# First expert stage: down product two chunks behind, a third hidden tile, waits per PSUM bank, and PSUM copies on ScalarE

## The reference

```python
shared_out = _swiglu(x, ws_gate, ws_up, ws_down)      # width 128
scores = sigmoid(x @ gate_weight.T)                   # 8 scores a token
topk_w, topk_idx = top_k(scores, 2)
topk_w = topk_w / (topk_w.sum(-1) + 1e-20) * 2.5
combine = einsum('tk,tke->te', topk_w, one_hot(topk_idx))
hmid = silu(x @ w_gate) * (x @ w_up)                  # 8 experts, width 64 each
out = einsum('te,teh->th', combine, hmid @ w_down) + shared_out
```

## Time and profile before

| | |
|---|---|
| runs of the kernel | 1990.7 us median of three (1988.94 to 1991.46) |
| profiled execution | 1989.05 us, of which the span of instructions is 1987.2 us |
| TensorE busy over the span | 81% |
| VectorE, ScalarE busy over the span | 71%, 50% |
| first experts in this execution | from 761.7 us, when its first ScalarE work starts, to 926.1 us, when its last statistics are done |
| mean granted TensorE clock over the span | 0.92 of full |

### The profile page before, as it was taken

How to read it: one execution, slowest core, us unless ns; L and a number is a source line. 1 busy time by engine, 2 the same in 40 slices (tenths; PEclk the granted TensorE clock), 3 DMA queues, 4 the chain that set the end, 5 groups by cost and what they waited for, 6 DMA issues and landing times. The chain is left out here.

```text
span 1987.2 us, 37884 instructions
## 1 busy us (share of the span) xinstructions
PE 1602.9 (81%) x11056; PEld 1044.5 (53%) x11056; DVE 1403.6 (71%) x3795; ACT 989.3 (50%) x2687; POOL 484.3 (24%) x503
## 2 busy tenths in 40 slices
PE   6999999999998997888967845776776433698998
PEld 3666666666664554555645744565665433243443
DVE  5777777777775665666864447999999855576775
ACT  3666666666663332333322258999999410111110
POOL 1111111111111010000001107888888551000000
PEclk9999999999999998998988977889888766799999
DMA  4111011110109100001660000000000000000000
GB/s 128 33 32 30 23 32 32 32 32 21 32 12 292 47 0 1 1 0 54 195 202 0 0 0 0 1 0 1 1 0 0 11 0 21 28 6 11 6 6 16
DMA packets 69349, 66.54 MB, mean 33 GB/s; under 512 B 5695, under 2 KB 66834, under 8 KB 69266
## 3 DMA queue, kind: packets, MB, share of 16 engines
q1 hardware_dynamic: 66598, 64.00, 10.7%
q10 hardware_dynamic: 2668, 1.62, 0.3%
HBM read 61.41 MB, written 4.19 MB: 33 GB/s over the span
## 5 line engine op out<-in xcount | busy, mean ns | idle before, releaser
L1962 PE MATMUL ss_y_ps<-ss_h,ss_diag 128*128 128x256 f32 x1024 | 266.1, 424 | 132.1 <-ACT sc_dt L1880 92.0
L1962 PEld LDWEIGHTS ss_y_ps<-ss_h,ss_diag 128*128 128x128 f32 x1024 | 217.2, 215 | 180.7 <-issue 93.9
L595 ACT ACTIVATE x_probs<-x_probs,x_neg_max 128x257 f32<-128x257 f32 x512 | 253.6, 498 | 63.2 <-DVE x_neg_max L696 63.2
L696 DVE CUSTOM_DVE_ANT_0 x_probs<-x_s_ps,x_mask_b 128x257 f32<-128x257 f32 x512 | 187.2, 422 | 132.6 <-PE x_s_ps L403 132.6
L1864 ACT ACTIVATE ss_decay<-sc_dt,sc_a 128x256 f32 (+1 forms) x496 | 207.1, 473 | 1.8 <-DVE ss_h L1927 1.8
L1918 DVE SCALAR_TENSOR_TENSOR ss_decay<-ss_decay,ss_h 128x1024 f32<-128x1024 f32 x124 | 152.3, 1228 | 29.3 <-ACT ss_decay L1864 29.1
L1874 ACT ACTIVATE ss_come<-ss_dtu,sc_xd 128x256 f32<-128x256 f32 x384 | 163.1, 507 | 6.6 <-POOL ss_dtu L1820 6.6
L1834 POOL TENSOR_TENSOR ss_diag<-all_ident,sc_xd 128x512 f32<-128x512 f32 x128 | 160.7, 1256 | 11.4 <-PE ss_y_ps L1962 1.4
L413 PE MATMUL x_pT_ps<-all_ident,x_probs 128*128 128x128 f32 x1024 | 162.0, 281 | 0.6 <-DVE x_pT L703 0.6
L703 DVE COPY x_pT<-x_pT_ps 128x512 f32<-128x512 f32 x256 | 161.2, 668 | 0.0
L1927 DVE CUSTOM_DVE_ANT_0 ss_h<-ss_come,ss_decay 128x1024 f32<-128x1024 f32 x124 | 149.9, 1209 | 0.0
(11 more groups left out here) (363 smaller groups left out, 3110.2 us busy)
## 6 DMA issues: line engine op xcount, KB each, us to landing
x_ctx_t<-ctxT SPq DMA_DIRECT2D x48, 514.0 KB, 3.8
kept_ctx_t<-ctxT SPq DMA_DIRECT2D x16, 514.0 KB, 7.9
kept_ctx_n<-ctx SPq DMA_DIRECT2D x16, 512.0 KB, 8.4
x_ctx_n<-ctx SPq DMA_DIRECT2D x16, 512.0 KB, 4.0
all_x<-x SPq DMA_DIRECT2D x4, 512.0 KB, 7.3
x_mid<-all_x SPq DMA_DIRECT2D x32, 64.0 KB, 3.8
all_x<-x_mid SPq DMA_DIRECT2D x4, 512.0 KB, 7.5
out<-all_x SPq DMA_DIRECT2D x8, 256.0 KB, 2.0
```

Source lines behind the costliest of these rows:

```text
L595: ins = nc.scalar.activation(probs[p][:, n, :], probs[p][:, n, :], ACT.Exp, scale=-1.0, bias=neg_max[p][:, n:n + 1], accum_out=sums[p][:, ...
L696: vec.tensor_tensor_reduce(probs[p][:, n, :], s_ps[:, c, 0:S2], mask_b[:, :], -1.0, -MASKED, ALU.add, ALU.min, neg_max[p][:, n:n + 1]).the ...
L1962: ins = nc.tensor.matmul(y_ps[p][:, 0:DI], diag[q][:, m, :], h[q][:, m, :], start=(q == 0 and m == 0), stop=(q == NQ - 1 and m == NH - 1))
```

## The change

- `project` stands two chunks behind (`LAG0 = 2`), and `hid` has three tiles.
- `up` is split into `gate_up` (G and U) and `weigh` (W). G raises a semaphore of its own, `gate_psum`, and waits for the silu of two chunks ago; U waits for the hidden tile of two chunks ago; W, or U where there is no W, raises `up_psum`. The wait for the next group's routing weights stands before W and no longer before G. ScalarE's silu waits for `gate_psum` and for the hidden tile of two chunks ago; VectorE's `hidden` waits for both `gate_sb` and `up_psum`.
- `copy_xT` and `copy_weights` run on ScalarE (activation Copy) in place of VectorE.
- `add_out` is split: the sum stands after chunk 1, the statistics (`moments`) after chunk 4.
- In group 0, G and U of chunks 0 and 1 are issued between `logits(0)` and `turn_weights(0)`.
- The groups are written out; there is no loop.

The diff, with unchanged parts left out:

```diff
-        hid = [sb(f"hid{p}", [P, TOK]) for p in range(2)]
+        hid = [sb(f"hid{p}", [P, TOK]) for p in range(3)]
...
+        gate_psum = sem("gate_psum")
+        LAG0 = 2
...
-            def up(n, p, h):
-                b = (p + h) % 2
+            def gate_up(i):
+                n, h, b = i // HC, i % HC, i % 2
+                if h == 0:
+                    pe.wait_ge(xT_sb, n + 1)
+                wait(pe, gate_sb, i - 1)
+                mm(g_ps[b][:, :], w_g[:, h, :], xnT[n % 2][:, :], start=True, stop=True).then_inc(gate_psum, 1)
+                wait(pe, hid_sb, i - 1)
+                ins = mm(u_ps[b][:, :], w_u[:, h, :], xnT[n % 2][:, :], start=True, stop=True)
+                if h == RC:
+                    ins.then_inc(up_psum, 1)
+
+            def weigh(i):
+                n, h, b = i // HC, i % HC, i % 2
                 if h == 0:
                     pe.wait_ge(wT_sb, n + 1)
-                wait(pe, hid_sb, n * HC + h - 1)
-                mm(g_ps[b][:, :], w_g[:, h, :], xnT[p][:, :], start=True, stop=True)
-                ins = mm(u_ps[b][:, :], w_u[:, h, :], xnT[p][:, :], start=True, stop=True)
                 if h < RC:
-                    ins = mm(w_ps[b][:, :], spread[:, h, :], weightT[p][:, :], start=True, stop=True)
-                ins.then_inc(up_psum, 1)
-
-            def project(n, p, h):
-                pe.wait_ge(hid_sb, n * HC + h + 1)
+                    mm(w_ps[b][:, :], spread[:, h, :], weightT[n % 2][:, :], start=True, stop=True).then_inc(up_psum, 1)
+
+            def project(i):
+                n, h = i // HC, i % HC
+                pe.wait_ge(hid_sb, i + 1)
                 if h == 0:
                     wait(pe, x_sb, n)
                 for k in range(GT):
-                    ins = mm(o_ps[:, k * D:(k + 1) * D], hid[(p + h) % 2][:, k * P:(k + 1) * P], w_d[:, h, :],
+                    ins = mm(o_ps[:, k * D:(k + 1) * D], hid[i % 3][:, k * P:(k + 1) * P], w_d[:, h, :],
                              start=(h == 0 and k == 0), stop=(h == HC - 1), skip_group_check=True)
                 ins.then_inc(down, 1)
 
...
             pe.wait_ge(g.experts_in, 16 * N_LOADS)
             turn_x(0)
-            logits(0, 0)
+            logits(0)
+            gate_up(0)
+            gate_up(1)
             turn_weights(0)
-            group(0, 0, False, True)
-            with pe.Fori(0, NG // 2 - 1) as i:
-                group(i * 2 + 1, 1, True, True)
-                group(i * 2 + 2, 0, True, True)
-            group(NG - 1, 1, True, False)
-            project(NG - 1, 1, HC - 1)
+            weigh(0)
+            weigh(1)
+            for n in range(NG):
+                for h in range(HC):
+                    if n * HC + h >= 2:
+                        gate_up(n * HC + h)
+                        weigh(n * HC + h)
+                    if n * HC + h >= LAG0:
+                        project(n * HC + h - LAG0)
+                    if n + 1 < NG:
+                        if h == 1:
+                            turn_x(n + 1)
+                        if h == 2:
+                            logits(n + 1)
+                        if h == 4:
+                            turn_weights(n + 1)
+            for i in range(NG * HC - LAG0, NG * HC):
+                project(i)
...
+            def copy_xT(n):
+                act.wait_ge(xT_psum, n + 1)
+                nc.scalar.activation(xnT[n % 2][:, :], m_ps[:, :], ACT.Copy).then_inc(xT_sb, 1)
+
             def sigmoids(n):
                 act.wait_ge(logits_psum, n + 1)
                 nc.scalar.activation(scores[:, :, 0:NE], m_ps[:, 0:GT * NE].rearrange("p (k e) -> p k e", k=GT),
                                      ACT.Sigmoid).then_inc(scores_sb, 1)
 
...
+            def copy_weights(n):
+                act.wait_ge(pads, 4)
+                act.wait_ge(wT_psum, n + 1)
+                nc.scalar.activation(weightT[n % 2][0:3 * NE, :], m_ps[0:3 * NE, :], ACT.Copy).then_inc(wT_sb, 1)
+
+            def silu(i):
+                act.wait_ge(gate_psum, i + 1)
+                wait(act, hid_sb, i - 1)
+                nc.scalar.activation(gate[i % 2][:, :], g_ps[i % 2][:, :], ACT.Silu).then_inc(gate_sb, 1)
+
+            norm_coefficients(nc, g, act, None, ln_step, lnw)
+            copy_xT(0)
+            sigmoids(0)
+            silu(0)
+            silu(1)
+            copy_weights(0)
+            for n in range(NG):
                 for h in range(HC):
-                    silu(n, p, h)
-                    if nxt and h == 2:
-                        sigmoids(n + 1)
-
-            norm_coefficients(nc, g, act, None, ln_step, lnw)
-            sigmoids(0)
-            with act.Fori(0, NG // 2 - 1) as i:
-                group(i * 2, 0, True)
-                group(i * 2 + 1, 1, True)
-            group(NG - 2, 0, True)
-            group(NG - 1, 1, False)
+                    if n * HC + h >= 2:
+                        silu(n * HC + h)
+                    if n + 1 < NG:
+                        if h == 1:
+                            copy_xT(n + 1)
+                        if h == 2:
+                            sigmoids(n + 1)
+                        if h == 4:
+                            copy_weights(n + 1)
...
             def norm(n):
+                wait(dve, xT_psum, n)
                 for k in range(GT):
                     t = n * GT + k
                     vec.tensor_scalar(xn[:, k, :], g.x[:, t, :], g.rstd[:, bass.ds(t, 1)], g.shift[:, bass.ds(t, 1)],
                                       ALU.mult, ALU.add).then_inc(xn_ready, 1)
-
-            def copy_xT(n, p):
-                dve.wait_ge(xT_psum, n + 1)
-                vec.tensor_copy(xnT[p][:, :], m_ps[:, :]).then_inc(xT_sb, 1)
...
+            def hidden(i):
+                b, d = i % 2, i % 3
+                dve.wait_ge(gate_sb, i + 1)
+                dve.wait_ge(up_psum, i + 1)
+                wait(dve, down, i - 2)
+                first = vec.tensor_tensor(hid[d][:, :], gate[b][:, :], u_ps[b][:, :], ALU.mult)
+                if i % HC < RC:
                     first.then_inc(mid_sb, 1)
-                    dve.wait_ge(mid_sb, n * RC + h + 1)
-                    vec.tensor_tensor(hid[b][:, :], hid[b][:, :], w_ps[b][:, :], ALU.mult).then_inc(hid_sb, 1)
+                    dve.wait_ge(mid_sb, i // HC * RC + i % HC + 1)
+                    vec.tensor_tensor(hid[d][:, :], hid[d][:, :], w_ps[b][:, :], ALU.mult).then_inc(hid_sb, 1)
                 else:
                     first.then_inc(hid_sb, 1)
 
             def add_out(n):
                 dve.wait_ge(down, n * HC + HC)
-                xs = g.x[:, bass.ds(n * GT, GT), :]
+                xs = g.x[:, n * GT:(n + 1) * GT, :]
                 vec.tensor_tensor(xs, xs, o_ps[:, :].rearrange("p (k d) -> p k d", k=GT), ALU.add).then_inc(x_sb, 1)
+
+            def moments(n):
                 dve.wait_ge(x_sb, n + 1)
                 for k in range(GT):
                     vec.bn_stats(g.bn[:, n * GT + k, :], g.x[:, n * GT + k, :]).then_inc(stats_sb, 1)
-
             norm(0)
-            copy_xT(0, 0)
             routing_top(0)
             routing_weights(0)
-            copy_weights(0, 0)
-            group(0, 0, False, True)
-            with dve.Fori(0, NG // 2 - 1) as i:
-                group(i * 2 + 1, 1, True, True)
-                group(i * 2 + 2, 0, True, True)
-            group(NG - 1, 1, True, False)
+            for n in range(NG):
+                for h in range(HC):
+                    hidden(n * HC + h)
+                    if n + 1 < NG:
+                        if h == 0:
+                            norm(n + 1)
+                        if h == 2:
+                            routing_top(n + 1)
+                        if h == 3:
+                            routing_weights(n + 1)
+                    if n and h == LAG0 - 1:
+                        add_out(n - 1)
+                    if n and h == 4:
+                        moments(n - 1)
             add_out(NG - 1)
+            moments(NG - 1)
             dve.wait_ge(stats_sb, T)
```

More of the change, by code:

```diff
@@ L1171, in turn_x, with logits @@
                 ins.then_inc(xT_psum, 1)
-            def logits(n, p):
+            def logits(n):
                 pe.wait_ge(xT_sb, n + 1)
                 for k in range(GT):
-                    ins = mm(m_ps[:, k * NE:(k + 1) * NE], xnT[p][:, k * P:(k + 1) * P], w_r[:, :], start=True, stop=True)
+                    ins = mm(m_ps[:, k * NE:(k + 1) * NE], xnT[n % 2][:, k * P:(k + 1) * P], w_r[:, :], start=True, stop=True)
                 ins.then_inc(logits_psum, 1)
@@ L1200, in project @@
                 for k in range(GT):
-                    ins = mm(o_ps[:, k * D:(k + 1) * D], hid[(p + h) % 2][:, k * P:(k + 1) * P], w_d[:, h, :],
+                    ins = mm(o_ps[:, k * D:(k + 1) * D], hid[i % 3][:, k * P:(k + 1) * P], w_d[:, h, :],
                              start=(h == 0 and k == 0), stop=(h == HC - 1), skip_group_check=True)
                 ins.then_inc(down, 1)
```

(35 more changed lines are left out.)

## The result

| | kernel before | changed kernel |
|---|---|---|
| median (range) of the runs of one comparison, us | 1989.82 (1987.5 to 1991.46), 4 runs | 1965.38 (1962.36 to 1966.9), 4 runs |
| time of the profiled execution, its span, us | 1989.05, 1987.2 | 1966.9, 1965.1 |
| the stage (from its first ScalarE table load to its last statistics), us | 164.37 | 141.42 |
| from its start to the first G of group 1, us | 32.10 | 28.37 |
| period, mean of six, us | 19.09 | 15.925 |

The ratio of the times is 0.9876, 95% interval 0.9859 to 0.9893: faster, by 24.4 us between the medians. The forecast was a gain of 22.8 and a time of 1967.9 us, with a range of 1963.0 to 1974.0.

What follows compares the result with a forecast made beforehand. TensorE, busy 87%, was nearest the limit, its idle time the prize: 11.9 us up to group 3 plus 12.4 over four periods, less 1.5 for the clock, is 22.8; 1990.7 - 22.8 = 1967.9 us, range 1963.0 to 1974.0.

Steps and rivals of the forecast that it cites:

- The pace and the period: Steady groups: TensorE's work 15.6 us; period from 19.0 to 15.9, with TW 0.2 late as the one wait.
- The three gaps: TensorE's waits before TX (1 us), TW (0.89) and the next group's first G (1.1) would go, but for TW's 0.2.
- 4 us in hand: Chunk latency: hidden ends at 3.54 and D, now two chunks later, comes at 7.6, so D never waits.
- I take the clock up at 772.0: Stage start: TensorE reaches 2.4 GHz at 772.0, earliest 770.2; first G of group 1 5.1 us sooner, bounds 6.6 and 3.1.
- a clock lost in the gap: The new 2.4 us TensorE gap in group 0 may drop the clock, costing 1.5 to 3.0 us; 1.5 taken.
- The loop written out I cost at nothing: Writing the groups out costs or gains nothing; bound 0.2 us at each of seven group changes either way.
- Rival 1: The routing chain sets the period at about 16.9: gain 17 us, time 1974, chance 0.14.
- Rival 2: The clock stays low through the stage's start and is lost again in the new gap: 1972 us, chance 0.08.
- Rival 3: Better: clock up early and never lost, period 15.6, gain 27.6, time 1963.1 us, chance 0.08.
- Rival 4: Slower: every added wait breaks TensorE's overlap, 120 x 0.26 = 31 us, slower by 8, 1999 us, chance 0.04.
- Rival 5: No change: Copy on ScalarE pulls in two table loads, 2.6 us twice a group, eating the gain; chance 0.02.
- the table rule: ScalarE's table switches: with a drain, 2.66 us each, the period would be 17.7 and the gain 12; not used.

Runs made afterwards that it cites:

- e9: Changed kernel with norm(1) right after group 0's routing and routing_weights ahead of hidden of chunk 3: 1958.54 us, ratio 0.9843.
- e2: Changed kernel with G of chunk 0 in groups 1 to 7 waiting for the turned weights again: 1970.32 us, ratio 0.9909.
- e3: Changed kernel with sum and statistics before norm, two hidden tiles and D one chunk behind: 1966.56 us, ratio 0.9889.
- e4: Changed kernel with the silu waiting for all products of its chunk again from chunk 2 on: 1969.54 us, ratio 0.9901.
- e12: Changed kernel, G waiting for turned weights, silu for all products, sum and statistics before norm, D one chunk behind, two tiles: 1981.11 us, ratio 0.995.
- e5: Changed kernel with two hidden tiles, D one chunk behind, both copies on VectorE and the sum ahead of norm: 1962.78 us, ratio 0.9869.
- e11: e5 run again: 1962.58 us, ratio 0.9871.
- e1: Changed kernel with two hidden tiles, D one chunk behind and both copies back on VectorE: 1966.38 us, ratio 0.9889.
- e7: Changed kernel with G and U of group 0's chunks 0 and 1 behind the turned weights again: 1966.91 us, ratio 0.9883.
- e6: e5 with groups 1 to 6 in a hardware loop of two groups a turn: 1964.31 us, ratio 0.9874.
- e8: Changed kernel with norm(1) right after the routing of group 0: 1961.15 us, ratio 0.9859.

## Why the prediction was right, and where it was not

**The pace and the period: right.** TensorE's work per group was put at 15.6, and e9, where it never waits between groups, shows 15.68. The 0.08 is one step: behind L, G to U takes 0.94 and not 0.86, in the kernel before too. By its letter the prediction's sign of being wrong (G to U longer than 0.86) is met there, but no added wait makes it. The period was put at 15.9 with TW 0.2 late as the one wait; it is 15.83 in four groups, with TW 0.14 late; the mean of six is 15.925. The other two have 0.2 and 0.36 more, from pauses in VectorE's written-out stream, of which this is one, in the changed kernel:

```profile
883.09 0.17 DVE L1107 COPY e_taken<-e_sorted 128x8 f32<-128x8 f32 x1
883.77 0.09 DVE L1099 MATCH_VALUE_LOAD e_marked<-e_taken,e_scores 128x8 f32 x1 [0.51 <-DVE e_taken L1107]
```

In other groups the second row comes 0.32 after the first, not 0.68. That TW has no slack was the prediction's reading too; it is why such a pause shows in the period at all.

**The three gaps: right, by e2 to e4 and e12.** Each is closed by the part of the change that the prediction named. What it did not see is that two of them depend on each other: with the silu late and the sum and statistics ahead of `norm`, TX is later than either alone makes it. Undoing one part at a time hides that.

**Which parts matter: half right.** The third tile and the lag were followed as part of the chunk's latency ("4 us in hand"), and the copies on ScalarE as if the period needed them. It needs neither, with the sum moved (e5, e11). That D of chunk 0 also waits for the old group's sum was in the text, at 8.05 with 1 us to spare; that the spare comes from the lag alone was left for e1 to show.

**The clock at the stage's start: mis-sized twice, with opposite signs.** "I take the clock up at 772.0" was 10.3 us after the stage's start; it rose 13.3 after it, near 778.0, 7.8 us into unbroken work that had begun at 770.20. So the first G after the gap came 18.63 us after the start against the forecast's 17.1, 1.5 late. The next paragraph charged 1.5 us for a clock lost in the gap, and no clock was lost. The first G of group 1 was thus forecast at 27.0 + 1.5 = 28.5 after the start and came at 28.37: right as a sum by luck, wrong in both terms. The forecast took a 2.9 us rise from one place, where TensorE had already been at its work for a while before a pause; e7 gives 4.3 for nearly the same work, and the changed kernel 7.8, or 6.1 from its first G. A single such row is no basis for a value. The Trainium skill ("TensorE: Matmul & The Clock Gate", What's actually happening) says that idling brings the slow state back, but not that every pause does. The 3.0 that the prediction drew from it for this gap does not follow, and the trace has 2.42 us of pause at a clock of 1.00.

**"The loop written out I cost at nothing": wrong.** Between e5 and e6 it is worth 0.34 a group, 2.0 in six, beyond the bound of 0.2 given. The reason was that TensorE streams over it; the cost is on VectorE, inside the chain that has no slack. This is hidden in the forecast because its sum was made from the measured 19.0, which holds the loop's cost, and from a new period counted without one.

**The rivals.** Rival 1, the routing chain as the limit at 16.9: not here, though e4 shows how near it is. Rival 2: its first half happened, its second did not. Rival 3 needed both halves of the start to go well; e9 reaches its period by another order. Rival 4 fell with D to G at 0.89 and G to U at 0.86 through the new waits. Rival 5 and the table rule fell on the rows of the routing in the changed kernel:

```profile
787.37 1.28 ACT L1259 ACT_TABLE_LOAD   x1
788.66 0.60 ACT L1259 ACTIVATE e_gate<-e_g_ps 128x512 f32<-128x512 f32 x1
```

The silu starts 0.01 after the reload is over (787.37 + 1.28 = 788.65), and Copy brings no load of its own: each group has two. The Trainium skill ("ScalarE: Activation LUTs", What ACT_TABLE_LOAD costs) adds a drain to each switch. From it the prediction estimated a period of 17.7; this row shows none, and the period is 15.925.

**The size.** The stage gained 22.95 against 22.8. Between the medians it is 24.4, between the profiled executions 22.15; the interval of the ratio allows 21.3 to 28.1. That the median came out 2.5 us under the forecast is inside that scatter, and no step of the prediction answers for it. Some of the fit is luck: the two clock terms at the stage's start nearly cancel, and so do the 2.98 us lost ahead of the stage and the 2.1 won behind it.

## What to carry to other kernels

Write TensorE's work of one period as a list of starts, hang every other engine's steps on it, and look for the waits that end last; with start-to-start times from rows of the same kernel, that gave a period right to 0.1 us. Several small waits between two groups can share one reserve of time: undo or remove them together as well as singly, and then ask which parts were not needed at all, since here three of the edits brought nothing that another place of the sum did not. When work moves into a pause, ask what stands behind it: the early chunks alone won 0.9 us, and 3.6 with the `norm(1)` behind them moved up as well, some 0.4 of it by the clock.

## What the runs showed of the hardware that I had not expected

- The granted clock rose 2.9 (before), 4.3 (e7) and 7.8 us (changed) into TensorE's unbroken work at the start of the same stage. e8 and e9, with one and the same order up to there, have 7.1 and 7.9, so the order alone does not decide it; what does stays open.
- A pause of 2.42 us on TensorE, right after the clock had risen, left it at 1.00.
- A hardware loop around the groups costs 0.34 us a group, in pauses of VectorE behind its own routing steps. The stream written out has pauses too, 0.2 to 0.5 us, but only in two groups of seven. Neither cause was found.
- TensorE's stream has three waits per chunk in place of two, and the one of `hidden` now stands between G and U. While they are satisfied they cost nothing that shows: D to G stays at 0.89, G to U at 0.86.
